# Two-layer cross-attention: the value product of the first layer from three 128-row matmuls per block to pairs of 64-row matmuls, with an accumulating transfer behind them

## What is computed

```python
q = hidden_state @ Wq + bq
k = encoder_hidden_state @ Wk + bk          # 8 key/value heads of 32
v = encoder_hidden_state @ Wv + bv
scores = einsum('bkgld,bksd->bkgls', q, k) * scale + mask
attn = softmax(scores, axis=-1)
out = einsum('bkgls,bksd->bkgld', attn, v)  # the changed product
x = out @ Wo + bo + hidden_state            # then a layer norm
```

## Time and profile before

| | before |
|---|---|
| median of 3 runs | 1744.62 us (1741.44 to 1746.93) |
| profiled execution, its own time | 1741.65 us |
| its span in the trace | 1739.8 us, mean granted TensorE clock 0.999 |
| PE busy | 1709.9 us, 98% |
| DVE busy | 1168.4 us, 67% |
| POOL busy | 1066.3 us, 61% |
| ACT busy | 581.0 us, 33% |
| chain that ended last | PE 66%, DVE 13%, POOL 10%, ACT 4%, DMA 2% |

### The profile page before, as it was taken

One profiled execution on the slowest core, in us unless ns is written; L12 is line 12 of the kernel. 1 busy time (PEld: TensorE's weight loads), 2 busy tenths in 40 slices (PEclk: granted clock), 3 DMA queues, 4 the chain that ended last, 5 costly groups with the idle time before them and its releaser, 6 DMA issues.

```text
span 1739.8 us, 22384 instructions
## 1 busy us (share of the span) xinstructions
PE 1709.9 (98%) x8449; PEld 1426.6 (82%) x8449; DVE 1168.4 (67%) x1106; ACT 581.0 (33%) x669; POOL 1066.3 (61%) x592
## 2 busy tenths in 40 slices
PE   6999999999999999999999999999999999999998
PEld 6888888888888788888888877888888888888887
DVE  7999898888988666565656578446644664466443
ACT  4444354444445433333434223122312231223110
POOL 1777877878788866575756553446734673467331
PEclk9999999999999999999999999999999999999999
DMA  8443244333236577777776856455545654565332
GB/s 239 104 111 86 77 110 108 78 80 78 74 96 165 180 241 228 229 230 224 240 221 223 263 177 194 170 169 182 172 154 170 186 167 155 170 172 180 132 109 97
DMA packets 278127, 280.11 MB, mean 161 GB/s; under 512 B 62330, under 2 KB 230404, under 8 KB 278020
## 3 DMA queue, kind: packets, MB, share of 16 engines
q1 hardware_dynamic: 276672, 276.97, 52.4%
q10 hardware_dynamic: 1348, 1.71, 0.3%
HBM read 175.81 MB, written 102.76 MB: 160 GB/s over the span
## 4 chain that ended last, share of the span: by engine, by line
PE 66%; DVE 13%; POOL 10%; issue 5%; ACT 4%; DMA 2%; SPq 0%; POOLq 0%; DVEq 0%; ACTq 0%
PE ps L53 21%; PE ps L54 21%; PE ps L55 21%; POOL pT0l L1382 3%; POOL pr L1386 2%; DVE small L1106 1%; PE ps L712 1%; PE ps L720 1%; DVE pT1r L1137 1%; DVE pT0r L1137 1%; DVE pr L1126 1%; ACT pT1h L880 1%; ACT pr L852 1%; DVE xT0r L1039 1%; POOL xb L1408 1%
## 5 line engine op out<-in xcount | busy, mean ns | idle before, releaser
L1459 POOL TENSOR_TENSOR x2Tl<-x2r,x2Th 128x1024 fp32r<-128x1024 f32 x31 | 74.5, 2403 | 274.6 <-ACT x2Th L972 274.6
L1236 DVE STREAM_TRANSPOSE x2r<-xd 128x1024 f32<-128x1024 f32 x32 | 68.8, 2148 | 199.9 <-PE ps L55 199.9
L1391 POOL TENSOR_TENSOR pr<-pr,small 128x1024 f32<-128x1024 f32 x64 | 121.9, 1905 | 95.0 <-DVE small L1132 94.9
L972 ACT CAST x2Th<-x2r 128x1024 fp32r<-128x1024 f32 x32 | 33.6, 1051 | 366.9 <-DVE x2r L1236 366.9
L1386 POOL TENSOR_TENSOR pr<-pr,small 128x1024 f32<-128x1024 f32 x64 | 121.9, 1905 | 8.4 <-DVE small L1110 6.0
L1408 POOL TENSOR_TENSOR xb<-xb,bo 128x1024 f32<-128x1024 f32 x32 | 76.9, 2403 | 72.6 <-DMA xb<-in_x_dram 72.6
L1106 DVE TENSOR_REDUCE small<-pr 128x16 f32<-128x1024 f32 x64 | 78.1, 1220 | 45.6 <-ACT pr L852 45.6
L1422 POOL TENSOR_TENSOR y<-y,bet 128x1024 f32<-128x1024 f32 x31 | 74.4, 2400 | 55.7 <-DVE y L1154 55.7
L1154 DVE TENSOR_TENSOR y<-y,gam 128x1024 f32<-128x1024 f32 x32 | 56.1, 1752 | 70.9 <-ACT y L893 70.9
L53 PE MATMUL ps<-wo0h,oc0l 128*128 128x512 f32 x256 | 102.3, 399 | 0.0
L53 PE MATMUL ps<-wo0h,oc1l 128*128 128x512 f32 x256 | 101.6, 397 | 0.4 <-DVE y L1191 0.4
(11 more groups left out here) (379 smaller groups left out, 5442.4 us busy)
## 6 DMA issues: line engine op xcount, KB each, us to landing
xr<-in_x_dram SPq DMA_DIRECT2D x128, 128.0 KB, 2.9
o_scratch<-ot SPq DMA_DIRECT2D x256, 64.0 KB, 1.8
ocr<-o_scratch SPq DMA_DIRECT2D x16, 1024.0 KB, 8.6
xb<-in_x_dram SPq DMA_DIRECT2D x32, 512.0 KB, 6.9
a_scratch<-ost SPq DMA_DIRECT2D x64, 256.0 KB, 3.5
b_scratch<-ost SPq DMA_DIRECT2D x64, 256.0 KB, 5.9
xd<-x_scratch SPq DMA_DIRECT2D x128, 128.0 KB, 2.9
raw<-b_scratch SPq DMA_DIRECT2D x64, 256.0 KB, 5.7
```

Source lines behind the costliest of these rows:

```text
L1236: nc.vector.transpose(x2r[:].rearrange("p k (t j) -> p t k j", t=TPB), xd[:].rearrange("p t (i k) -> p t k i", k=KT)).then_inc(x2_turned, 1)
L1391: nc.gpsimd.tensor_tensor(heads(v), heads(v), mx.unsqueeze(2).to_broadcast([P, TPB * GRP, KEYS]), ALU.subtract)\
L1459: nc.gpsimd.tensor_tensor(x2T[1][:], x2r[:], f32(x2T[0][:]), ALU.subtract).then_inc(x2_lo, 1)
```

## The change

It does these things:

1. `vb` now holds V for pairs of heads: heads 0 and 1 lie in the rows 0 to 63, heads 2 and 3 in the rows 64 to 127, and in the columns the block diagonal of V's high part (64 columns) stands beside that of its low part (64 columns).
2. The value product of a unit becomes eight matmuls of 64 rows and 512 moved columns in four pairs: for each key half c and each part x of the probabilities, one matmul for the rows 0 to 63 into one PSUM bank and one for the rows 64 to 127 into the other. Both banks are now used by every unit, so PE waits for the copy of unit v-1 (before: v-2). The product low by low is now contained.
3. In each bank the rows 0 to 63 hold the part from V's high part and the rows 64 to 127 that from its low part. ACT's copy covers both banks (128x1024, before 128x512) into a wider `ot`.
4. POOL starts, one slot later and as the first thing in its slot, a transfer from `ot`'s rows 64 to 127 onto its rows 0 to 63 that adds (64 rows of 4 KB). It waits for `o_ev`; SP's stores now wait for this transfer (`o_sum`) and stand one slot later.
5. To make room in SBUF, `qs` has one buffer in place of two (ACT's write of the high part waits for the scores of the unit before), and the second `ot` lies where the second layer's `wT` low part comes; DVE waits for the stores at that point.
6. The low part of the first chunk's quarters moves from POOL (slots 30, 34, 38, 42) to DVE (one slot later each), and the low part of the probabilities of unit 62 moves from POOL's slot 65 to the end of DVE's slot 64.

```diff
+def summed_in(u):
+    if 5 <= u < UNITS + 3:
+        return [u - 5] if u < UNITS + 2 else [u - 5, u - 4]
+    return [u - 4] if u == UNITS + 3 else []
...
-        qs = [[at(f"qs{i}{x}", 152 + 4 * i + 2 * j, [P, TPB, P], F32R) for j, x in enumerate("hl")] for i in range(2)]
+        qs = [at(f"qs{x}", 152 + 2 * j, [P, TPB, P], F32R) for j, x in enumerate("hl")]
-        vb = [at(f"vb{i}", 164 + 2 * i, [P, 2, 2, P], F32R) for i in range(2)]
+        vb = [at(f"vb{i}", 164 + 2 * i, [P, 2, 2, 2, HD0], F32R) for i in range(2)]
-        ot = [at(f"ot{i}", 202 + 2 * i, [P, BLK]) for i in range(2)]
+        ot = [at(f"ot{i}", o, [P, 2, BLK]) for i, o in enumerate((202, 156))]
...
 SP, slot(u):
-                if 4 <= u < UNITS + 4:
-                    v = u - 4
-                    sp.wait_ge(o_ev, v + 1)
+                for v in summed_in(u):
+                    sp.wait_ge(o_sum[v % 2], 16 * (v // 2 + 1))
                     for a in range(4):
                         sp.dma_start(...ot[v % 2]...).then_inc(o_st[v % 2], 16)
...
 PE, values_of(v):
-                    after(pe, o_ev, v - 1)
-                    for c in range(2):
-                        last = three(nc, V[v % 2], ...)
+                    after(pe, o_ev, v)
+                    for n, (c, x) in enumerate(((0, 1), (0, 0), (1, 1), (1, 0))):
+                        for h in range(2):
+                            rows = slice(64 * h, 64 * (h + 1))
+                            last = nc.tensor.matmul(V[h], vb[v % 2][rows, c].rearrange("p x a d -> p (x a d)"),
+                                                    pT[v % 2][x][rows, c].rearrange("p j n -> p (j n)"), start=n == 0, stop=n == 3)
...
 ACT, slot(u):
-                    nc.scalar.copy(ot[v % 2][:].rearrange("p (j i m) -> p j i m", j=GRP, m=TPB),
-                                   V[v % 2].rearrange("p (j m i) -> p j i m", j=GRP, m=TPB)).then_inc(o_ev, 1)
+                    nc.scalar.copy(ot[v % 2][:].rearrange("p h (j i m) -> p (h j) i m", j=GRP, m=TPB),
+                                   VV.rearrange("p (j m i) -> p j i m", j=2 * GRP, m=TPB)).then_inc(o_ev, 1)
-                    after(act, scores, u - 1)
+                    after(act, scores, u)
...
 DVE, end of slot(u):
+                if (i := chunk0(u - 1)) is not None:
+                    dve.wait_ge(oc_hi, i + 1)
+                    nc.vector.tensor_tensor(oT[0][1][:, 2 * i:2 * i + 2], ..., ALU.subtract).then_inc(oc_lo, 1)
+                if u == UNITS:
+                    v = UNITS - 2
+                    dve.wait_ge(p_hi, v + 1)
+                    nc.vector.tensor_tensor(pT[v % 2][1][:], pTr[v % 2][:], f32(pT[v % 2][0][:]), ALU.subtract).then_inc(p_lo, 1)
...
 POOL, slot(u):
+                for v in summed_in(u):
+                    pool.wait_ge(o_ev, v + 1)
+                    nc.gpsimd.dma_start(ot[v % 2][:64], ot[v % 2][64:], accum_op=ALU.add).then_inc(o_sum[v % 2], 16)
-                if 3 <= u < UNITS + 3:
+                if 3 <= u < UNITS + 3 and u != UNITS + 1:
...
-                if (i := chunk0(u)) is not None:
-                    chunk_lo(0, i, 2)
```

26 lines of the change are left out of this document (15 added, 11 removed).

## The result

The changed kernel takes **1756.32 us** (median of 4, 1755.53 to 1756.78) against 1744.32 for the kernel before (median of 4, the three runs of the table and one more, 1741.44 to 1746.93): ratio 1.007, 95% interval 1.0058 to 1.0083. That is 12 us slower. My range, 1737 to 1763, held it, but my forecast, 1741 and no measurable change, was wrong. The spans in the traces are those of single executions, 1739.8 and 1753.7.

The account below looks back on a forecast made before the run. PE was taken to set the pace, by 0.5% over a chain of DVE, POOL and ACT. Terms -2.2 + 0 + 0.5 - 2.8 + 0.9 = -3.6 us gave 1738 by the profiled execution, 1741 as median; range 1737 to 1763.

Parts of the forecast that it names:

- Value matmuls: PE's value product: pairs save 0.45 us, switching tiling costs 0.42 a visit; net 0.03 a unit, -2.2 us in all.
- POOL's transfer: Head of each POOL slot: an issue of 0.8 us, hidden in even slots, adds 0 us.
- the window: POOL in even slots, between centering and low part: 1.08 us in which the transfer's issue costs nothing.
- The rival to which I gave a third: POOL's issue exceeds 1.08 us between centering and low part in even slots: 1752 to 1761 us; chance 0.33.
- 0.08 from a single pair: Steady slots: the DVE, POOL and ACT chain runs 0.08 us a pair of slots faster than PE.
- Chunk quarters: Four chunk slots: low parts moved from POOL to DVE return 0.7 of 1.04 us lost at each, -2.8 us.
- The wait for the copy: PE waits for unit v-1's copy, grown from 0.56 to about 1.05 us; PE slips once, +0.5 us.
- at worst +3: SP's stores wait for a transfer issued some 5 us earlier: 0, or +3 us if it lands later.
- Seam: Units 62 and 63: PE's product for unit 63 at 589.4 in place of 588.54, +0.9 us.
- comes in time: Seam: unit 62's low part on DVE is ready for PE, 3.6 us earlier than on POOL.
- No wait of PE for unit 62: Sign expected in the trace after: PE doesn't wait for unit 62, but several us ahead of unit 63.

Follow-up runs that it names:

- The longer slot: Changed kernel with six small fills (128x40) on POOL behind each issue of the transfer: 1761.41 us, ratio 1.0112.
- with these two put right as well: Changed kernel without the transfer, ACT's splits of x and Wo behind the copy, unit 62's low part back on POOL: 1739.41 us.
- the kernel with ACT's order: Changed kernel with ACT's splits of x and Wo behind the slot's copy of the values: 1751.78 us, ratio 1.005.
- the four with SP's or POOL's order changed: Changed kernel: Wo loads before stores, slot-64 loads after, 1759.38; with ACT's splits behind the copy: stores first 1755.32, also Wk1/Wv1 later 1756.91, POOL's seam reordered 1753.75.
- the two runs with the stores first: Changed kernel, ACT's splits behind the copy, SP's stores ahead of all loads in the slot: 1755.32 us; Wk1/Wv1 load also moved to slot 66: 1756.91.
- SP's order: Changed kernel with Wo's loads ahead of the stores in slots 56 to 59 and unit 59's store ahead of slot 64's loads: 1759.38 us.

## Why the prediction was wrong

**Value matmuls**, -2.2: the mechanism holds, the size doesn't (and 64 times the 0.03 us I had would have been -1.9). PE's timeline, changed kernel, has 0.32 and 0.34 into the pairs, 0.23 and 0.24 between them and 0.33 out:

```profile
431.69 0.39 PE L55 MATMUL ps<-xT0h,wq0h 128*128 128x512 f32 x1
432.01 0.50 PE L641 MATMUL ps<-pT0l,vb 64*128 64x512 f32 x2
432.35 0.40 PE L641 MATMUL ps<-pT0h,vb 64*128 64x512 f32 x2
432.58 0.40 PE L641 MATMUL ps<-pT0l,vb 64*128 64x512 f32 x2
432.82 0.40 PE L641 MATMUL ps<-pT0h,vb 64*128 64x512 f32 x2
433.15 0.50 PE L53 MATMUL ps<-xT0h,wq0l 128*128 128x512 f32 x1
```

With the 0.34 that follows, a visit takes 1.80 us from the matmul ahead of it on; eight distances of 0.227 took 1.82. Ten slots went from 82.61 to 82.59 us, so 64 give about 0.1: what is saved on the matmuls goes at the switch.

**POOL's transfer**, 0: right on POOL, with 0.84 us for my 0.8 and the window kept. The rival to which I gave a third, an overrun of it, didn't happen. The longer slot showed where it would have: 0.98 us still fit ahead of the low part of an even slot, not the 0.58 of an odd one. There the 0.40 us too much came out as 0.23 a pair, so I estimate that the chain of DVE, POOL and ACT had 0.17 us of room, where I had read 0.08 from a single pair (16.45; five pairs from 417.32 to 499.69 average 16.47).

**Chunk quarters**, -2.8: right in kind; 3.4 here, 4.0 in the kernel before.

**The wait for the copy**, +0.5 and "at worst +3": the step that failed. I priced the closer wait by steady slots, where it is indeed free, and the stores by a landing of 5 us with a slot to spare. I didn't ask what the copy stands behind in the few slots that aren't steady, and took the landing for a constant. In the trace the transfers land after 3.4 to 8.6 us, three of the 64 after more than 5, two of these (8.6 and 5.8) at the seam; and the time to spare was being used in the steady slots already, as the even units show (1.1 us left of 3.9). PE waited 12.3 us for the copy in six places, for my 0.5, and ran at the lower clock after two of them, against a loss of 13.9 in all.

It holds two things, which the runs separate in part. The closer wait alone, in the kernel before, costs 0 to 1 us. The transfer alone is worth 8 us by the medians (12.0 above the kernel before with it, 4.2 without), 8.6 by the spans. The rest is the closer wait together with what stands ahead of the copy, 3.5 us at unit 57, and unit 62's low part on DVE: with these two put right as well the loss is gone (-3.4 in span, -3.8 by the medians).

A rule of the Trainium skill that I passed over speaks of the closer wait: Perfetto Trace Analysis, section Matmuls, wants independent groups of matmuls to rotate through PSUM banks, so that one's evacuation overlaps the next one's matmuls. The pairs give that up; by the run with the wait alone this costs nothing here while the copy is on time, and by the 12.3 us much once it isn't. Another is on the landing: DMA: Bandwidth & Descriptors (the Trainium skill), section Anatomy of one DMA — SWDGE (gpsimd) path, fits 2.0 us plus the bytes over 436 KB per us, by which I estimate 2.6 us for these 256 KB. The trace has 3.7 at the median, beside other traffic, and 8.6 at the most.

**Seam**, +0.9: followed POOL and ACT and left out SP's queue. POOL did wait for the copy, as forecast (0.97 us at 593.38), but ACT's copies waited for stores first, 6.12 us, which I hadn't looked for, and V of unit 62 came late as well. That unit 62's low part "comes in time" on DVE, 3.6 us earlier, was wrong too: beside POOL's add it takes 3.14 us, in the kernel before it gained 1.0, and the chain of unit 63 pays. The place of the second `ot`, which I gave no price, holds DVE for 2.54 us. "No wait of PE for unit 62" was my sign to look for; it waited 5.78 us there.

**Open** is how the last 8 us (seam and tables) divide between the two `ot` buffers, POOL's late issue, SP's waiting and the traffic (DMA share 0.47 for 0.28 in the steady slots). From unit 61 to 640 us the changed kernel loses 8.1 us, the kernel with ACT's order 6.9, and the four with SP's or POOL's order changed 7.7 to 11.4, each at another place; without the transfer it is 3.5. The traces show what came last each time: the copy of unit 61 in the changed kernel (with V of unit 62 only 1.8 us ahead of its end), V of unit 62 in the two runs with the stores first, and, where both came in time (SP's order), the stores of unit 60, whose transfer POOL issues 10 to 12 us after the copy. Not tried: issuing that one earlier, and a third `ot` buffer, for which I found no room in SBUF.

## What to carry to other kernels

A transfer put into a chain costs its issue on one engine and its landing everywhere else: follow it to the buffer that it keeps, to the queue that waits for it in order, and to the loads behind that queue. Take the landing where traffic is densest and not at the median, and where a wait has no name in the profile, compare its end with the landings of the loads. When a ring loses a slot of slack, steady slots tell nothing; list the slots in which the waited-for instruction stands behind something rare, a weight load, a chunk, the end of a stage, and price those. And try each part of a bundled change alone: the one useful part here, four subtractions moved off the pacing chain, gave 4 us in the traces and had nothing to do with the rest.
